# GpSimd normalises the head outputs ahead of k's low parts, q's high part comes two exponentials later, and the maxima's rows are copied from one head's block

## The chip, the cores and the metric

The kernel runs on one core of a Trainium2 chip. The metric is the device time of one execution in microseconds. Before the change it is 1233.8 us (median of three runs, 1231.41 to 1234.8).

## The reference

A transformer block on x (16 sequences of 256 tokens, 512 wide) with cross-attention to ctx, then a feed-forward net with simulated quantisation:

```
q = rope(layernorm(x) @ wq.T); k = rope(ctx @ wk.T); v = ctx @ wv.T     # 16 heads of 32
scores = q_h @ k_h.T * sqrt(32), -inf where |query - key| > 128
x = x + softmax(scores) @ v_h -> (256, 512) @ wo.T + wo_b
h = gelu(quant16(layernorm(x)) @ quant8(W_in) + b_in)                   # 2048 wide, erf gelu
out = x + quant16(h) @ quant8(W_out) + b_out
```

quant16 scales by the largest absolute value of the whole tensor, quant8 by that of each hidden unit in the weights.

## The kernel before, in words

Each engine has its own instruction stream, written out by hand, and semaphores between them. Work on one engine is done strictly in the order written, a wait included.

**Part one, attention**, is 16 steps, one per sequence (`step(b, ...)`, one function per engine). In step b three sequences are in the works: the scores and softmax of b, the projections of b + 1, and the output product and residual of b − 1. Products are done in three terms of high and low parts (`split3`), so each operand has a `_hi` (a rounded copy by ScalarE) and a `_lo` (the rest, by VectorE or GpSimd).

- First half of a step, TensorE: scores of 16 heads two at a time (L604), between them the k, q and v products of b + 1 (L521 to L523) and the transposes of normalised x (`x_transposes`, L533). VectorE takes the row maxima of each head (L1191) and between them the reciprocals of the softmax denominators of b − 1 (`invert`, L1232, out to `neg_max`, whose memory it shares as `den_r`), t_lo for x (L1224), the rotation of k (L1214 to L1217) and the normalisation of oT (`normalise`, L1238).
- The shares: SyncE stores the reciprocals to DRAM (L356), waits for that, and loads them spread over the partitions into `share` (L359), which lies in the first two slots of `probs`. oT times share is the normalised head output. ScalarE rounds it to t_hi (`ot_lead`, L937), GpSimd takes the rest, t_lo (`ot_rest`, L1516), and TensorE multiplies both with wo (`o_products`, L588).
- Middle: VectorE negates the row maxima and splits them (`split_max`, L1196 and L1198), TensorE takes four output products and then transposes the maxima (L616), ScalarE copies them in two pieces to the rows MROW and up of `q_st` for heads 0 to 3 (`max_copy`, L953), and SyncE copies those rows to the other 12 heads (`stack_max`, L350).
- Second half, TensorE: transposed scores (L638, two matmuls per head) with the remaining output products between them, and after heads 7, 11 and 15 and at the end a clump of weighted sums (L652) and denominators (L665) for four heads. ScalarE: 16 exponentials (L960), and among them the high part of q for b + 1 (L906) and of ctx for b + 2 (L911). GpSimd: a band mask on each exponential (`band`, L1528), and among them q's four low parts (L1505) and ctx's four (L1511). VectorE: rotation of q, residual, layer-norm sums, a row block of W_in quantised, layer norm of x for b + 2, the largest value (`largest`, L1162).
- SyncE's queue in step b: load x_res (L325), the shares (L356, L359), x (L319), the maxima's rows, then, once k's low parts and later q's low parts are done, the stacks of k and q for b + 1 (L343; 24 transfers), a block of W_in (L333) and ctx (L315) among them, and the store of x1 (L329). The next step's x_res waits until that store has landed.

GpSimd in the first half: wo_b onto x_res (`bias_x`, L1521), k's low parts (L1505), t_lo.

**Part two** multiplies by W_in and takes the gelu. **Part three** multiplies by W_out: per chunk of 128 hidden units ScalarE scales (L1109) and rounds (L1100), VectorE makes integers (L1459) and the low part g_lo (L1483), TensorE does eight matmuls (L857), and GpSimd adds b_out to four blocks of each tile of x1 (`bias_tile`, L1568).

Of the kernel before, what the change touches and what calls it, by code (L numbers as in the profile page):

```python
# [29 lines left out]
P = 128  # L30
# [55 lines left out]
def build(nc, t):  # L86
# [12 lines left out]
    with ExitStack() as ctx:  # L99
# [212 lines left out]
        def _(sp):  # L312
# [33 lines left out]
            def stack_max(b):  # L346

                sp.wait_ge(mT_done, MAX_COPIES * (b + 1))
                for i in range(1, NC4):
                    sp.dma_start(q_st[MROW:P, KC * i:KC * (i + 1)].bitcast(F32),  # L350
                                 q_st[MROW:P, 0:KC].bitcast(F32)).then_inc(max_stacked[i - 1], 16)

# [164 lines left out]
        def _(pe):  # L517
# [7 lines left out]
            def x_transposes(j, s):  # L525

                if s == 0:
                    pe.wait_ge(ln1_norm, 2 * j + 2)
                    wait(pe, wt_done, j - 1)
                    wait(pe, den_done, j - 1)  # L530
                    wait(pe, rope_step["q"], ROPE_OPS * j)
                for c in range(KC):
                    mm = pe.transpose(q_bank[s][:, c * P:(c + 1) * P], x_ln[:, s, c * P:(c + 1) * P], ident[:])  # L533
                mm.then_inc(xt_mm, 1)
# [365 lines left out]
        def _(act):  # L900
# [95 lines left out]
            def step(b, par, has_c, has_o, has_proj, has_xt):  # L996
# [14 lines left out]
                for n in range(H):  # L1011
                    softmax_exp(b, n)
                    if n == 4 and has_proj:
                        split_hi("q", b + 1)
                    if n == 8 and has_xt:
                        ctx_hi(b + 2)
# [117 lines left out]
        def _(dve):  # L1134
# [59 lines left out]
            def split_max(b):  # L1194
                dve.wait_ge(max_done, 2 * H * (b + 1))
                dve.tensor_scalar(neg_max[:, :, MROW:MROW + H].bitcast(F32R), row_max[:], -1.0, None, ALU.mult).then_inc(msplit, 1)  # L1196
                dve.wait_ge(msplit, 2 * b + 1)
# [32 lines left out]
            def invert(b):  # L1230
                dve.wait_ge(den_mm, NC4 * (b + 1))
                dve.reciprocal(den_r, den_bank[:, 0:S]).then_inc(den_done, 1)  # L1232

            def normalise(b, half):
                dve.wait_ge(oT_out, 2 * b + half + 1)
                dve.wait_ge(share_in, 16 * (b + 1))
                part = oT[:, 2 * half:2 * half + 2].rearrange("p i t -> p (i t)")
                dve.tensor_tensor(part, part, share[:, 2 * half * S:2 * (half + 1) * S], ALU.mult).then_inc(onorm, 1)  # L1238

# [62 lines left out]
            def step(b, par, has_c, has_o, has_proj, has_xt):  # L1302

                between = {p: [] for p in range(H // 2)}
                if has_o:
                    between[0] += [lambda: invert(b - 1)]
                    between[5] += [lambda: normalise(b - 1, 0), lambda: normalise(b - 1, 1)]
                if has_proj:
# [191 lines left out]
        def _(pool):  # L1500
# [12 lines left out]
            def ot_rest(j, s):  # L1513
                pool.wait_ge(ot_hi, 2 * j + s + 1)
                tok = slice(s * P, (s + 1) * P)
                pool.tensor_tensor(t_lo[:, :, tok], oT[:, :, tok], t_hi[:, :, tok].bitcast(F32), ALU.subtract).then_inc(ot_lo, 1)  # L1516

            def bias_x(j):
                pool.wait_ge(xres_in, 16 * (j + 1))
                for s in range(2):  # L1520
                    pool.tensor_tensor(x_res[:, s], x_res[:, s], wo_b[:], ALU.add).then_inc(xres_b, 1)  # L1521
# [14 lines left out]
            def step(b, par, has_c, has_o, has_proj, has_xt):  # L1536
                if has_o:
                    bias_x(b - 1)
                if has_proj:
                    for c in range(KC):  # L1540
# [4 lines left out]
                for n in range(H):  # L1545
                    band(b, n)
                    if 4 <= n < 8 and has_proj:
                        split_lo("q", b + 1, n - 4)
                    if n in (8, 9, 10, 11) and has_xt:
                        ctx_lo(b + 2, n - 8)  # L1550

# [13 lines left out]
            def bias_tile(i, par):  # L1565
                pool.wait_ge(xc_in[par], 8 * i + (16 if par == 0 else 8))
                for u in range(SUB):
                    pool.tensor_tensor(xq[:, par, u], xq[:, par, u], b_out[:], ALU.add).then_inc(xc_b, 1)  # L1568

# [33 lines left out]
```

## Time and profile before

| | us |
|---|---|
| median of three runs | 1233.8 |
| the profiled execution | 1233.87 |
| its span in the trace | 1232.2 |
| TensorE busy | 1148.4 (93%) |
| VectorE busy | 984.4 (80%) |
| ScalarE busy | 640.7 (52%) |
| GpSimd busy | 367.7 (30%) |

The mean granted TensorE clock is 0.985 of full. TensorE's and VectorE's shares are means over three parts. In the 572 us from 128 to 700 of the span, which hold steps of part one alone, TensorE is busy for 537.79 us and VectorE for 507.73, ScalarE for 259.83 and GpSimd for 261.33. In the last 248 us (part three) they are busy for 237.46, 200.91, 177.83 and 48.86. Matmuls are pipelined, so that busy TensorE is not TensorE at its peak. What releases an engine at each step is to be read from the waits and the chain, not from these shares.

### The profile page before, as it was taken

Reading aid. Unit: us, or ns where it says so; the run is one execution under the profiler, and the core shown is the slowest. Engines: PE = TensorE matmul, PEld = TensorE weight load, DVE = VectorE, ACT = ScalarE, POOL = GpSimd, SP = SyncE. Lnnn points to the kernel's source line nnn. Section 1 sums busy time; section 2 is a strip of 40 time slices with the busy share of each in tenths; the row PEclk is TensorE's granted clock in tenths of the full one; section 3 lists DMA queues with packets and bytes.
Section 4 is the critical chain, followed back from the end, with each engine's and each line's share of the span. In section 5 each row is a group of like instructions: output and inputs, shape, how many; then the busy total and the mean of one; then the engine's idle time right before and its main releaser. Section 6 shows DMA issues by size and latency. Waiting matters only on the chain.

```text
span 1232.2 us, 23572 instructions
## 1 busy us (share of the span) xinstructions
PE 1148.4 (93%) x7884; PEld 770.6 (63%) x7928; DVE 984.4 (80%) x2541; ACT 640.7 (52%) x1001; POOL 367.7 (30%) x540
## 2 busy tenths in 40 slices
PE   6989999999999999999999767999999989999998
PEld 6867777876787787687677545444444444444443
DVE  6868889989888988988988746666666688888886
ACT  5254355345335434534533433655556457777775
POOL 1135346345434624634553331000000030121230
PEclk9989999999999999999999969999999999999999
DMA  8463574565466456457545622555554400677762
GB/s 270 124 143 108 162 180 128 143 176 146 126 176 159 121 151 180 131 141 193 132 122 142 180 82 77 175 207 202 203 195 145 150 4 30 186 223 236 239 223 95
DMA packets 95916, 191.12 MB, mean 155 GB/s; under 512 B 13377, under 2 KB 24769, under 8 KB 95809
## 3 DMA queue, kind: packets, MB, share of 16 engines
q1 hardware_dynamic: 95808, 189.75, 52.2%
q8 instruction: 60, 0.98, 0.4%
q14 instruction: 48, 0.39, 0.1%
HBM read 89.16 MB, written 43.91 MB: 108 GB/s over the span
## 4 chain that ended last, share of the span: by engine, by line
DVE 35%; PE 35%; issue 24%; DMA 2%; ACT 1%; SPq 1%; POOL 0%; DVEq 0%; POOLq 0%; ACTq 0%
PE bank L857 17%; DVE bank L1191 7%; PE bank L521 4%; PE bank L522 4%; PE bank L523 4%; DVE bn L1137 3%; DVE roped L1217 2%; DVE rt L1214 2%; PE bank L604 2%; DVE rt L1215 2%; DVE row_max L1191 2%; DVE neg_max L1232 2%; DVE x_res L1184 2%; PE bank L533 1%; DVE nt_t L292 1%
## 5 line engine op out<-in xcount | busy, mean ns | idle before, releaser
L1191 DVE CUSTOM_DVE_ANT_0 bank<-bank,mask 128x256 f32<-128x256 f32 x512 | 201.6, 455 | 52.1 <-PE bank L604 45.3
L857 PE MATMUL bank<-wout_int,g_lo 128*128 128x512 bf16 x512 | 193.5, 379 | 1.1
L857 PE MATMUL bank<-wout_int,g_hi 128*128 128x512 bf16 x491 | 185.7, 379 | 4.3 <-DVE g_lo L1483 4.0
L818 PE MATMUL bank<-qT_lo,win_int 128*128 128x512 bf16 x496 | 188.0, 379 | 1.2
L818 PE MATMUL bank<-qT_hi,win_int 128*128 128x512 bf16 x474 | 179.6, 379 | 0.0
L960 ACT ACTIVATE probs<-bank 128x512 f32<-128x512 f32 x256 | 142.9, 603 | 50.4 <-PE bank L638 46.1
L1528 POOL TENSOR_SCALAR_AFFINE_SELECT probs<-probs 128x256 f32<-128x256 f32 x256 | 109.9, 433 | 82.8 <-ACT probs L960 79.1
L1483 DVE TENSOR_TENSOR g_lo<-h_int,g_hi 128x512 f16<-128x512 f32 x128 | 104.2, 814 | 34.4 <-ACT g_hi L1100 34.0
L604 PE MATMUL bank<-k_st,q_st 96*128 96x256 f32 x512 | 97.7, 303 | 22.6 <-DVE row_max L1191 20.9
L1521 POOL TENSOR_TENSOR x_res<-x_res,wo_b 128x512 f32<-128x512 f32 x32 | 42.0, 1334 | 237.6 <-DMA x_res<-in_x 230.2
L638 PEld LDWEIGHTS bank<-q_st,k_st 128*128 128x128 f32 x512 | 91.2, 194 | 31.0 <-issue 13.6
L1068 ACT ACTIVATE h_ring<-bank,b_in,g_scale 128x512 f32<-128x512 f32 x96 | 73.1, 779 | 71.2 <-PE bank L818 54.1
L1425 DVE TENSOR_REDUCE hmax<-h_ring 128x512 f32 (+1 forms) x96 | 63.4, 683 | 57.3 <-ACT h_ring L1068 55.0
L638 PE MATMUL bank<-q_st,k_st 128*128 128x256 f32 x512 | 104.7, 295 | 2.3 <-ACT probs L960 1.1
L604 PEld LDWEIGHTS bank<-k_st,q_st 96*128 96x128 f32 x512 | 75.8, 193 | 47.4 <-DVE row_max L1191 33.0
L1100 ACT CAST g_hi<-h_int 128x512 f16<-128x512 f32 x128 | 78.9, 617 | 42.6 <-PE bank L857 31.1
L1568 POOL TENSOR_TENSOR xq<-xq,b_out 128x512 f32<-128x512 f32 x32 | 48.5, 1546 | 154.2 <-DMA xq<-x_scratch 147.0
L857 PEld LDWEIGHTS bank<-wout_int,g_hi 128*128 128x128 f16 x512 | 50.0, 98 | 66.3 <-issue 6.4
L857 PEld LDWEIGHTS bank<-wout_int,g_lo 128*128 128x128 f16 x512 | 50.1, 98 | 59.8 <-DVE g_lo L1483 0.2
L652 PE MATMUL bank<-probs,v_sb 128*32 128x256 f32 x1024 | 69.4, 388 | 18.1 <-ACT probs L960 12.0
L818 PEld LDWEIGHTS bank<-qT_lo,win_int 128*128 128x128 bf16 x496 | 48.5, 98 | 57.8
L818 PEld LDWEIGHTS bank<-qT_hi,win_int 128*128 128x128 bf16 x496 | 48.5, 98 | 57.7
(170 smaller groups left out, 2712.9 us busy)
## 6 DMA issues: line engine op xcount, KB each, us to landing
hidden_scratch<-h_ring SPq DMA_DIRECT2D x96, 256.0 KB, 2.0
h_ring<-hidden_scratch SPq DMA_DIRECT2D x96, 256.0 KB, 2.9
k_st<-k_hi SPq DMA_DIRECT2D x128, 128.0 KB, 2.6
q_st<-q_hi SPq DMA_DIRECT2D x128, 128.0 KB, 2.4
xq<-x_scratch SPq DMA_DIRECT2D x16, 1024.0 KB, 6.1
x_ln<-in_x SPq DMA_DIRECT2D x16, 512.0 KB, 4.6
ctx_raw<-in_ctxT SPq DMA_DIRECT2D x16, 512.0 KB, 5.0
k_st<-k_lo SPq DMA_DIRECT2D x64, 128.0 KB, 2.8
```

What stands on the lines that cost most here:

```text
L604: mm = pe.matmul(ring[n % 2][:, qb * S:(qb + 1) * S], q_st[0:MROW, n, qb * P:(qb + 1) * P], k_st[0:MROW, n], start=True, stop=True)
L638: mm = pe.matmul(third[n][:, kb * S:(kb + 1) * S], k_st[:, n, kb * P:(kb + 1) * P], q_st[:, n], start=True, stop=True)
L652: mm = pe.matmul(pv_bank[i // 2][DK * c:DK * (c + 1), (i % 2) * S:(i % 2 + 1) * S], v_sb[:, par, kb, n], probs[:, n % SLOTS, kb], start=kb ...
L818: mm = pe.matmul(bank[f % 4][:], win_int[:, c, f * P:(f + 1) * P], part[:, par, c], start=c == 0 and part is qT_hi, stop=c == KC - 1 and p ...
L857: return pe.matmul(bank[4 * par + u][:], part[:, f % 4, u * P:(u + 1) * P], wout_int[:, f], start=f == 0 and part is g_hi, stop=f == FC - ...
L960: act.activation(probs[:, n % SLOTS].rearrange("p k q -> p (k q)"), third[n][:], ACT.Exp, scale=SCORE_SCALE).then_inc(exp_done, 1)
L1068: act.activation(dst, bank[f % 4][:], ACT.Gelu, bias=b_in[:, f:f + 1], scale=g_scale[:, f:f + 1]).then_inc(gelu_done, 1)
L1100: act.copy(g_hi[:, f % 4], h_int[:, f % 4]).then_inc(ghi_done, 1)
L1191: dve.tensor_tensor_reduce(sc, sc, mask[:, (1 - qb) * P:(1 - qb) * P + S], 1.0, NEG, ALU.add, ALU.max, row_max[:, qb, n:n + 1]).then_inc(m ...
L1425: dve.tensor_reduce(hmax[:, bass.ds(FC * n + f, 1)], src, AX_X, ALU.max, apply_absolute_value=True).then_inc(hmax_done, 1)
L1483: dve.tensor_tensor(g_lo[:, f % 4], h_int[:, f % 4], g_hi[:, f % 4], ALU.subtract).then_inc(glo_done, 1)
L1528: pool.affine_select(out=far, in_=far, compare_op=ALU.is_ge, fill=0.0, base=1 - P, pattern=[[0, 2], [1, P]], channel_multiplier=1).then_in ...
```

## The change

1. The normalisation of oT by the shares goes from VectorE (behind head 11's row maxima) to GpSimd, between `bias_x` and k's low parts. VectorE's `split_max` gets an explicit wait for the store of the reciprocals, as both use `neg_max`.
2. ScalarE makes q's high part behind exponential 6 in place of 4, ctx's behind 9 in place of 8; GpSimd's q low parts go behind bands 6 to 9 (from 4 to 7), ctx's behind 10 to 13 (from 8 to 11).
3. The first half of x's transposes no longer waits for the reciprocal; the second does, whose bank it is.
4. `stack_max` waits only for the first of ScalarE's two copies and reads head 0's rows four times over, in place of reading heads 0 to 3.
5. In part three each of GpSimd's adds of b_out waits for a chunk of its own, 6, 8, 10 or 12 of the tile.

```diff
             def stack_max(b):
-                sp.wait_ge(mT_done, MAX_COPIES * (b + 1))
+                sp.wait_ge(mT_done, MAX_COPIES * b + 1)
                 for i in range(1, NC4):
                     sp.dma_start(q_st[MROW:P, KC * i:KC * (i + 1)].bitcast(F32),
-                                 q_st[MROW:P, 0:KC].bitcast(F32)).then_inc(max_stacked[i - 1], 16)
+                                 q_st[MROW:P, 0:1].bitcast(F32).to_broadcast([P - MROW, KC, S])).then_inc(max_stacked[i - 1], 16)
...
                 if s == 0:
                     pe.wait_ge(ln1_norm, 2 * j + 2)
                     wait(pe, wt_done, j - 1)
+                    wait(pe, rope_step["q"], ROPE_OPS * j)
+                else:
                     wait(pe, den_done, j - 1)
-                    wait(pe, rope_step["q"], ROPE_OPS * j)
...
-                    if n == 4 and has_proj:
+                    if n == 6 and has_proj:
                         split_hi("q", b + 1)
-                    if n == 8 and has_xt:
+                    if n == 9 and has_xt:
                         ctx_hi(b + 2)
...
             def split_max(b):
                 dve.wait_ge(max_done, 2 * H * (b + 1))
+                wait(dve, den_out, 16 * b)
...
-            def normalise(b, half):
-                dve.wait_ge(oT_out, 2 * b + half + 1)
-                dve.wait_ge(share_in, 16 * (b + 1))
-                part = oT[:, 2 * half:2 * half + 2].rearrange("p i t -> p (i t)")
-                dve.tensor_tensor(part, part, share[:, 2 * half * S:2 * (half + 1) * S], ALU.mult).then_inc(onorm, 1)
...
-                    between[5] += [lambda: normalise(b - 1, 0), lambda: normalise(b - 1, 1)]
...
+            def normalise(j, half):
+                pool.wait_ge(oT_out, 2 * j + half + 1)
+                pool.wait_ge(share_in, 16 * (j + 1))
+                part = oT[:, 2 * half:2 * half + 2].rearrange("p i t -> p (i t)")
+                pool.tensor_tensor(part, part, share[:, 2 * half * S:2 * (half + 1) * S], ALU.mult).then_inc(onorm, 1)
...
                 if has_o:
                     bias_x(b - 1)
+                    normalise(b - 1, 0)
+                    normalise(b - 1, 1)
...
-                    if 4 <= n < 8 and has_proj:
-                        split_lo("q", b + 1, n - 4)
-                    if n in (8, 9, 10, 11) and has_xt:
-                        ctx_lo(b + 2, n - 8)
+                    if 6 <= n < 10 and has_proj:
+                        split_lo("q", b + 1, n - 6)
+                    if 10 <= n < 14 and has_xt:
+                        ctx_lo(b + 2, n - 10)
...
                 for u in range(SUB):
+                    pool.wait_ge(hint_done, FC * i + 6 + 2 * u)
                     pool.tensor_tensor(xq[:, par, u], xq[:, par, u], b_out[:], ALU.add).then_inc(xc_b, 1)
```

GpSimd's instructions of one step, from the residual's bias on (x_res; k_lo and q_lo are low parts, t_lo is that of oT, AFFINE_SELECT is the band of one head). Before:

```order
L1521 TENSOR_TENSOR x_res<-x_res,wo_b 128x512 x2
L1505 TENSOR_TENSOR k_lo<-roped,k_hi 128x256 x4
L1516 TENSOR_TENSOR t_lo<-oT,t_hi 128x4x128 x2
L1528 AFFINE_SELECT probs<-probs 128x256 x5
L1505 TENSOR_TENSOR q_lo<-roped,q_hi 128x256
```

And after the change, whose line numbers differ:

```order
L1522 TENSOR_TENSOR x_res<-x_res,wo_b 128x512 x2
L1517 TENSOR_TENSOR oT<-oT,probs 128x512 x2
L1500 TENSOR_TENSOR k_lo<-roped,k_hi 128x256 x4
L1511 TENSOR_TENSOR t_lo<-oT,t_hi 128x4x128 x2
L1529 AFFINE_SELECT probs<-probs 128x256 x7
L1500 TENSOR_TENSOR q_lo<-roped,q_hi 128x256
```

The two multiplications of oT by the shares (in `probs`) now stand ahead of k's low parts, and seven bands instead of five ahead of q's first low part.

ScalarE's instructions in the second half of a step, from the maxima's two copies into q_st. Before:

```order
L953 CAST q_st<-bank 32x512 x2
L960 ACTIVATE probs<-bank 128x512 x5
L906 CAST q_hi<-roped 128x1024
L960 ACTIVATE probs<-bank 128x512 x4
L911 CAST cT_hi<-ctx_raw 128x1024
```

And after:

```order
L954 CAST q_st<-bank 32x512 x2
L961 ACTIVATE probs<-bank 128x512 x7
L907 CAST q_hi<-roped 128x1024
L961 ACTIVATE probs<-bank 128x512 x3
L912 CAST cT_hi<-ctx_raw 128x1024
```

q's rounding moved behind two more exponentials, ctx's behind one more.

## Rows read from the trace of the kernel before

**Rows 1.** The page, chain that ended last, by engine

```profile
DVE 35%; PE 35%; issue 24%; DMA 2%; ACT 1%; SPq 1%; POOL 0%; DVEq 0%; POOLq 0%; ACTq 0%
```

**Rows 2.** Line L1232: duration ns min/median/max, first and last start

```profile
L1232 DVE RECIPROCAL neg_max<-bank x15: 1752/1753/1758, 86.9 to 699.7; 128x256 f32<-128x256 f32 x15
```

**Rows 3.** Chain that ended last, 390 to 440: start us, us, what

```profile
411.06 0.14 DVE oT L1238
...
434.11 0.73 DVE dmax L1162 x2
...
436.93 1.62 DVE neg_max L1232
```

**Rows 4.** TensorE in order of time: start, us, instructions, [idle before, releaser]

```profile
395.18 1.06 PE L533 MATMUL bank<-ident,x_ln 128*128 128x128 f32 x8 [0.47 <-DVE neg_max L1232]
...
414.31 0.47 PE L588 MATMUL bank<-wo_hi,t_hi 128*128 128x512 f32 x1
...
415.87 0.44 PE L616 MATMUL bank<-ident,neg_max 128*128 128x128 f32 x2 [0.39 <-DVE neg_max L1198]
...
422.50 1.07 PE L652 MATMUL bank<-probs,v_sb 128*32 128x256 f32 x16 [0.80 <-ACT probs L960]
...
432.42 1.07 PE L652 MATMUL bank<-probs,v_sb 128*32 128x256 f32 x16 [0.33 <-POOL probs L1528]
```

**Rows 5.** GpSimd in order of time: q's last low part in three steps

```profile
250.28 0.74 POOL L1505 TENSOR_TENSOR q_lo<-roped,q_hi 128x256 fp32r<-128x256 f32 x1
...
425.49 0.74 POOL L1505 TENSOR_TENSOR q_lo<-roped,q_hi 128x256 fp32r<-128x256 f32 x1
...
469.11 0.74 POOL L1505 TENSOR_TENSOR q_lo<-roped,q_hi 128x256 fp32r<-128x256 f32 x1
```

**Rows 6.** SyncE's queue: issue of the shares' load behind each of these

```profile
274.14 0.58 SPq L359 DMA_DIRECT2D probs<-den_scratch  x1
...
447.03 0.58 SPq L359 DMA_DIRECT2D probs<-den_scratch  x1
...
491.87 0.58 SPq L359 DMA_DIRECT2D probs<-den_scratch  x1
```

**Rows 7.** Line L359, the shares' load

```profile
DMA to landing us min/median/max: 3.4/3.8/4.6
```

**Rows 8.** VectorE in order of time, the normalisation

```profile
410.91 1.29 DVE L1238 TENSOR_TENSOR oT<-oT,probs 128x512 f32<-128x512 f32 x2
```

**Rows 9.** GpSimd in order of time, k's low parts and the first t_lo

```profile
408.00 2.83 POOL L1505 TENSOR_TENSOR k_lo<-roped,k_hi 128x256 fp32r<-128x256 f32 x4 [1.71 <-ACT k_hi L906]
412.93 1.27 POOL L1516 TENSOR_TENSOR t_lo<-oT,t_hi 128x512 fp32r<-128x512 f32 x1 [2.11 <-ACT t_hi L937]
```

**Rows 10.** Line L1521: duration ns min/median/max

```profile
L1521 POOL TENSOR_TENSOR x_res<-x_res,wo_b x32: 1262/1292/1760, 95.0 to 750.8; 128x512 f32<-128x512 f32 x32
```

**Rows 11.** Part three: TensorE's waits (page and timeline), VectorE's integers

```profile
L857 PE MATMUL bank<-wout_int,g_hi 128*128 128x512 bf16 x491 | 185.7, 379 | 4.3 <-DVE g_lo L1483 4.0
...
1016.69 0.38 PE L857 MATMUL bank<-wout_int,g_hi 128*128 128x512 bf16 x1 [1.19 <-DVE g_lo L1483]
...
1050.65 0.48 DVE L1459 TENSOR_SCALAR h_int<-h_int,wout_man 128x512 f32<-128x512 f32 x1
...
1054.45 1.49 DVE L1459 TENSOR_SCALAR h_int<-h_int,wout_man 128x512 f32<-128x512 f32 x1
```

**Rows 12.** ScalarE in order of time, exponentials 5 to 7

```profile
421.76 1.57 ACT L960 ACTIVATE probs<-bank 128x512 f32<-128x512 f32 x3
```

**Rows 13.** VectorE in order of time, the last step's normalisation

```profile
718.82 1.29 DVE L1238 TENSOR_TENSOR oT<-oT,probs 128x512 f32<-128x512 f32 x2 [8.38 <-DMA probs<-den_scratch]
```

**Rows 14.** Step 0: TensorE's wait; windows of 5 us, PEclk after POOL's column

```profile
64.72 0.44 PE L616 MATMUL bank<-ident,neg_max 128*128 128x128 f32 x2 [2.08 <-DVE neg_max L1198]
...
65.00:70.00 5.00, 3.90 (x16) 3.21 (x14) 4.76 (x9) 3.77 (x8) 1.91 (x4) 0.52 0.47 105
70.00:75.00 5.00, 4.27 (x35) 2.08 (x34) 4.16 (x11) 2.38 (x4) 4.42 (x8) 0.50 0.60 136
```

## The prediction

> **What bounds the kernel now.** I read the page first. Its chain of what ended last is 35% VectorE and 35% TensorE, with GpSimd at 0% [rows 1]. The kernel has three parts: attention, about 745 us of the span in 16 steps, the first feed-forward product, and the second. The change lies in the attention steps and, by one wait, in the last part. The starts of the 15 reciprocals of the denominators stand 14 steps apart, from 86.9 to 699.7, which gives 43.8 us per step [rows 2]. I take the step around 393 to 437 as the pattern.
>
> Next I read the chain inside that step [rows 3]. It runs through VectorE's tail behind the row maxima (the last work is `largest` at 434.1) to the next reciprocal at 436.9; from a reciprocal it passes to TensorE's transposes of x, which waited for it (395.18) [rows 4], along TensorE, and back into VectorE's row maxima, with the normalisation of oT inside at 411. So VectorE and TensorE hand over to each other. TensorE's own waits in a step are small [rows 4]: 0.47 us for the reciprocal, 0.39 us for the negated maxima ahead of their transposes (they start at 415.87; I call this moment M), 0.80 us for an exponential, 0.33 us for GpSimd's last band.
>
> Last I looked for a loop which isn't on that chain but is almost as long. GpSimd ends q's last low part at 425.49 + 0.74 = 426.2 [rows 5]; then SyncE's queue issues q's stacks, one weight row block, ctx, more stacks, the store of x1, and behind it the load of x_res, the reciprocals' store and, once that has landed, the broadcast load of the shares, at 447.03 [rows 6], which lands in a median 3.8 us [rows 7]. So the shares are in 447.0 + 3.8 − 426.2 = 24.6 us behind q's low parts. In the step after it is 491.87 + 3.8 − 469.85 = 25.8, and in the worst step 274.14 + 3.8 − 251.0 = 26.9 [rows 5, 6]. I take 25.5. Today the normalisation starts at 410.9 [rows 8], and the shares of that step landed before it (the step after: 447.0 + 3.8 = 450.8, against 410.9 + 43.6 = 454.5), so there are 3.7 us of slack, and 3.7 − (26.9 − 24.6) = 1.4 in the worst step. The profile does not show this slack as a wait; the question is whether the change eats it.
>
> **The change part by part.**
>
> *Normalisation to GpSimd.* VectorE loses two instructions, 1.2 us per step [rows 3, 8]. GpSimd gains two 128x512 instructions with two SBUF inputs. The nearest row is its own t_lo, 1.27 us each [rows 9]; its add of x_res and wo_b goes from 1.26 to 1.76 [rows 10]. Bounds 2.5 and 3.5 us for the pair; I take 2.55, since beside it VectorE only runs row maxima. They are put ahead of k's four low parts (2.83 us) on an engine that works in order, and behind these comes t_lo [rows 9]. What follows the landing of the shares was 1.3 (VectorE, both halves) + 0.7 (ScalarE's t_hi, which GpSimd's t_lo waited for) + 1.3 (first t_lo) = 3.4 us with the semaphores. It becomes 2.55 + 2.83 + 1.27 + 0.15 = 6.8 us, because k's low parts can't start before the shares are in. t_hi on ScalarE hides behind k's low parts. TensorE's first output product needs this first t_lo: it starts at 414.31, right at t_lo's end at 414.2 [rows 4, 9].
>
> In a sentence of its own: the Trainium skill (SBUF — State Buffer, "Who interferes with whom") says that a VectorE instruction with at most one SBUF input does not contend with GpSimd, and one with two does. By it the row maxima (one PSUM, one SBUF input) leave the pair at 2.5; if they did contend as in the 1.76 row, it would be 3.5 and the sum 13 us more. Rows bear out the contention at least: with GpSimd's add beside it, VectorE's 0.48 us tensor_scalar took 1.49 [rows 11].
>
> *q's high part behind exponential 6.* It starts 0.98 us later (two exponentials at a pitch of 0.49, three of them in 1.57) [rows 12], and GpSimd's q_lo, and with it SyncE's whole queue, start later too. GpSimd does the bands of 5 and 6 ahead, which it had to do between before, so q's last low part ends about 0.75 us later, 11.1 us behind M instead of 10.36 (426.23 − 415.87). Bounds 0 and 0.98. TensorE's wait of 0.80 for exponential 5 goes, but the last clump then waits for GpSimd's band 15, today's end of 432.4 [rows 4], whose engine has the same work: it ends some 0.15 us earlier, so that is what remains of the 0.80. ctx's later low parts end just as SyncE's queue comes to its load: no charge.
>
> *x transposes.* The first half no longer waits for the reciprocal; by the time of the second it is ready: 0.47 us of TensorE's wait gone.
>
> *Maxima's rows.* The three copies can be issued after ScalarE's first copy, half a microsecond sooner, in 1 KB pieces in place of 4 KB. The nearest broadcast load lands in 3.4 to 4.6 us [rows 7]; scores need it about 3 us after issue, so it costs between 0 and 1 us a step, and I take 0, because it moves a quarter of the bytes of that load. The wait of the negation for den_out is long fulfilled: 0.
>
> *Bias in the last part.* TensorE waits 4.0 us in all for g_lo there, 1.19 us at a time, while GpSimd adds two tiles' bias in a row [rows 11]. Spread over the chunks, these waits go: −4 us (bounds 0 and −4).
>
> **The sum.** Loop one, TensorE and VectorE: 43.8 − 0.47 − 0.15 and about 0.5 of the 1.2 us of normalisation (the rest is lost since TensorE still has v's products there) gives 42.65. Loop two, M to M: 11.1 + 25.5 + 6.8 + 1.05 (four output products ahead of the transposes) = 44.45 us. The second is longer, and longer than today's 43.8, so it sets the step: 0.65 × 13 = +8.5. The first step with a normalisation still gains 1.2. The last step waits 8.38 us for the shares today [rows 13], with nothing to hide in: +0.75 for q and +1.3 for the slower engine, +2. The last part −4. Together +5.3: this is the profiled execution's 1233.9 (its span is 1232.2) to 1239, and that execution stands within 0.1 us of the median 1233.8.
>
> But in this loop TensorE stands idle in front of the output products: today it is through its scores 414.31 − 372.25 = 42.1 us behind the last M (43.62 us before this one), then 42.1 − 0.47 − 0.15 − 0.7 = 40.7 (0.7 for its own waits on the row maxima behind the normalisation), and t_lo comes at 11.1 + 25.5 + 6.8 = 43.4: 2.7 us, 1.8 to 4.1 by the step. In step 0 it waited 2.08 us at this same place, and the granted clock was at half (0.52 and 0.50, 1.2 of 2.4 GHz) for the next 10 us [rows 14]. A fall would hit the output products and the transposed scores, some 7 us of TensorE work that is then on the loop. Bounds per fall 0 and 7; I take 3, as TensorE has no gaps there and the clock came back under work in rows 14. I expect four falls in 13 steps, where the idle time is above average: +12. Forecast 1251.
>
> A sentence apart: the Trainium skill (TensorE: Matmul & The Clock Gate, "Part 1: The HAM clock gate") calls the half rate the default that activity lifts; what rows 14 show agrees.
>
> **The rivals.**
> 1. *Faster.* The queue loop is shorter than I make it, by 1.5 us or more (transfers land sooner when they fall in quieter stretches, or q's low parts end no later), so the first loop sets the step: 42.65, −1.1 × 14 = −15, and −4: 1215. For it: of today's slack of 1.4 to 3.7 us most steps have 2.5 or more. Against it: 0.75 + 3.4 us are added. If the loop is only 0.7 shorter, it is 1228.
> 2. *The loop, but no fall of the clock*: 1239. For it: TensorE's waits of 0.3 to 0.8 us in each step do not move the clock, and it is not shown where between these and 2.08 it falls. Against it: step 0.
> 3. *The clock falls in nearly every step*: 1239 + 13 × 3 = 1278. For it: each step has the same idle place. Against it: half of them are shorter than step 0's.
> 4. *No change that counts*: the added 0.65 per step is 0, and the gains of the last part meet the last step's loss, 1232.
>
> **How the numbers follow.** Forecast 1251 with 0.42, rival 1 0.20, rival 2 0.20, rival 3 0.10, rival 4 0.08. The range is 1224 to 1275: it takes in rival 2 and 4 and the near half of rival 1, and stops short of 3; the likeliest case's own range is 1242 to 1264. Within 0.3% (3.7 us, about what a measurement of this kernel can tell from no change) is rival 4 and a little of the others: 0.10; faster 0.20, slower 0.70.
>
> **What would show it.** Right: steps of 44.4 us or more; GpSimd waits for the shares, TensorE's idle time ahead of L588 is named and ends with GpSimd's t_lo, VectorE has idle time in its row maxima, and the granted clock dips in some steps. Also no wait over 1 us for g_lo in the last part. Wrong: steps of 42.7 us, with the chain still through VectorE's tail, or a share that lands before 24 us. If q's last low part ends at M + 10.4, that step was wrong alone.

## The result, and the profile after

| | before | after |
|---|---|---|
| median | 1233.55 us (1231.41 to 1234.8, 4 runs) | 1251.11 us (1246.93 to 1256.15, 4 runs) |
| ratio after / before | | 1.0142, 95% interval 1.0117 to 1.0168 |
| profiled execution, its span | 1233.9, 1232.2 | 1256.15, 1254.3 |
| reciprocal to reciprocal, mean of 14 steps | 43.77 | 45.46 |
| mean granted clock, 128 to 680 | 1.00 | 0.98 |

The change makes the kernel 17.6 us slower; 1251 was forecast. The profiled execution of after is the longest of its four, 5 us above the median. It also has the lowest mean granted clock over its whole span, 0.971; the other three have 0.974, 0.974 and 0.977. So its steps show more of the loss than the median has.

The page's chain of what ended last, by engine; beside [rows 1], VectorE has fallen from 35% to 28%, and DMA and SyncE's queue have grown from 2% and 1%:

```profile
PE 38%; DVE 28%; issue 24%; DMA 4%; SPq 3%; POOL 1%; ACT 1%; DVEq 0%; POOLq 0%
```

The line of the reciprocals, which answers to [rows 2]. (722.8 − 86.4) / 14 gives 45.46 us per step:

```profile
L1234 DVE RECIPROCAL neg_max<-bank x15: 1750/1752/1756, 86.4 to 722.8; 128x256 f32<-128x256 f32 x15
```

The chain inside a step, where before it was VectorE's tail [rows 3]. It now runs through the queue's transfers and GpSimd's normalisation to TensorE's output products (start us, us, what):

```profile
315.39 4.56 DMA x_scratch<-x_res
...
320.45 3.87 DMA den_scratch<-neg_max
...
324.34 3.53 DMA probs<-den_scratch
...
328.01 2.54 POOL oT L1517 x2
...
331.73 2.88 issue
334.60 2.05 PE bank L589 x4
```

The 2.88 us of "issue" are TensorE's wait, in which GpSimd does k's low parts and the first t_lo.

GpSimd in order of time, from the end of one step into the next: q's last low part, then the work behind the shares. The columns are those of [rows 4]:

```profile
438.93 0.73 POOL L1500 TENSOR_TENSOR q_lo<-roped,q_hi 128x256 fp32r<-128x256 f32 x1
...
464.53 2.52 POOL L1517 TENSOR_TENSOR oT<-oT,probs 128x512 f32<-128x512 f32 x2 [1.64 <-DMA probs<-den_scratch]
467.01 2.81 POOL L1500 TENSOR_TENSOR k_lo<-roped,k_hi 128x256 fp32r<-128x256 f32 x4
469.78 2.51 POOL L1511 TENSOR_TENSOR t_lo<-oT,t_hi 128x512 fp32r<-128x512 f32 x2
```

TensorE at the output products and the transposes of the negated maxima (M), in that step and in the one before it:

```profile
427.08 0.47 PE L589 MATMUL bank<-wo_hi,t_hi 128*128 128x512 f32 x1 [2.37 <-issue]
...
428.33 0.44 PE L617 MATMUL bank<-ident,neg_max 128*128 128x128 f32 x2
...
471.15 0.47 PE L589 MATMUL bank<-wo_hi,t_hi 128*128 128x512 f32 x1 [1.25 <-issue]
472.62 0.44 PE L617 MATMUL bank<-ident,neg_max 128*128 128x128 f32 x2 [0.30 <-DVE neg_max L1200]
```

M to M is 472.62 − 428.33 = 44.3 us, and its pieces can be read off: 439.66 − 428.33 = 11.3 from M to the end of q's last low part; 464.53 − 439.66 = 24.9 to the start of the normalisation, 0.14 us behind the landing of the shares; 471.15 − 464.53 = 6.6 to the first output product; 1.47 to the next M. GpSimd stood idle 1.64 us for the shares, TensorE 1.25 to 2.37 us for GpSimd. In before no engine waited for the shares but in the last step. The shares' load itself lands as before (us, min/median/max), beside [rows 7]:

```profile
DMA to landing us min/median/max: 3.4/3.8/5.1
```

The same waits added up over the whole program (us, times, longest):

```profile
PE bank L589 <- issue: 31.6, 14, 3.9
POOL oT L1517 <- DMA probs<-den_scratch: 23.9, 15, 3.0
```

So TensorE stands 31.6 / 14 = 2.26 us per step in front of the output products. "issue" names no releaser, but each of these waits ends as the first t_lo ends.

The granted clock, in windows of 5 us (columns as in [rows 14]) around the longest of these waits, 3.9 us, and in the step after it:

```profile
285.00:290.00 5.00, 2.07 (x8) 1.78 (x9) 4.80 (x10) 0.96 (x3) 4.07 (x5) 0.90 0.00 0
290.00:295.00 5.00, 5.00 (x23) 4.25 (x23) 3.03 (x5) 3.13 (x7) 1.51 (x4) 0.76 0.35 82
330.00:335.00 5.00, 1.36 (x7) 1.10 (x7) 4.45 (x14) 1.62 (x3) 5.00 (x7) 0.83 0.00 0
335.00:340.00 5.00, 5.00 (x16) 4.02 (x16) 3.42 (x6) 1.66 (x3) 0.74 (x1) 0.50 0.16 39
```

TensorE works 2.07 and 1.36 of 5 us, and the clock then goes to half (1.2 of 2.4 GHz). There are eight such falls between step 0 and the last, each in or behind one of the waits, of 2.08 to 3.94 us. Two waits of 2.28 and 2.37 us have none behind them, nor have the waits of 1.92 us and less.

The last step, GpSimd and TensorE, beside [rows 13]. The wait for the shares is 1.60 us now, but the first output product comes 25.49 us behind the reciprocal, where it came 22.64 behind before:

```profile
743.74 2.48 POOL L1517 TENSOR_TENSOR oT<-oT,probs 128x512 f32<-128x512 f32 x2 [1.60 <-DMA probs<-den_scratch]
...
748.31 0.77 PE L589 MATMUL bank<-wo_hi,t_hi 128*128 128x512 f32 x1 [11.80 <-ACT t_hi L938]
```

The last part is better, as meant. In place of the 4.3 us of [rows 11] TensorE waits 0.4 us:

```profile
L858 PE MATMUL bank<-wout_int,g_hi 128*128 128x512 bf16 x491 | 185.8, 379 | 0.4 <-issue 0.2
```

### The profile page after: what moved, and what is told of

It is laid out like the page before. It is cut to its first block, busy times and chain, and to the rows that moved or that the text cites. A ratio compares the mean times of both kernels' runs of the same rounds, so it can differ in the third digit from the quotient of the medians.

```text
span 1254.3 us, 23605 instructions
## 1 busy us (share of the span) xinstructions
PE 1154.3 (92%) x7884; PEld 779.9 (62%) x7928; DVE 985.3 (79%) x2511; ACT 641.3 (51%) x1001; POOL 395.6 (32%) x570
## 4 chain that ended last, share of the span: by engine, by line
PE 38%; DVE 28%; issue 24%; DMA 4%; SPq 3%; POOL 1%; ACT 1%; DVEq 0%; POOLq 0%
PE bank L858 17%; DVE bank L1192 4%; PE bank L589 4%; PE bank L521 3%; PE bank L522 3%; PE bank L523 3%; DVE bn L1138 3%; SPq L343 2%; DVE roped L1219 2%; PE bank L605 2%; PE bank L639 2%; DVE rt L1217 2%; DVE rt L1216 2%; DVE nt_t L292 1%; DVE neg_max L1234 1%
## 5 line engine op out<-in xcount | busy, mean ns | idle before, releaser
L1529 POOL TENSOR_SCALAR_AFFINE_SELECT probs<-probs 128x256 f32<-128x256 f32 x256 | 106.8, 421 | 89.5 <-ACT probs L961 85.1
L1522 POOL TENSOR_TENSOR x_res<-x_res,wo_b 128x512 f32<-128x512 f32 x32 | 43.8, 1390 | 254.8 <-DMA x_res<-in_x 247.4
L1478 DVE TENSOR_TENSOR g_lo<-h_int,g_hi 128x512 f16<-128x512 f32 x128 | 89.1, 696 | 41.4 <-ACT g_hi L1101 37.8
L639 PEld LDWEIGHTS bank<-q_st,k_st 128*128 128x128 f32 x512 | 94.1, 197 | 31.3 <-issue 13.6
L1101 ACT CAST g_hi<-h_int 128x512 f16<-128x512 f32 x128 | 78.9, 617 | 47.2 <-PE bank L858 43.1
L1572 POOL TENSOR_TENSOR xq<-xq,b_out 128x512 f32<-128x512 f32 x32 | 41.5, 1296 | 166.5 <-ACT h_int L1110 166.5
L589 PE MATMUL bank<-wo_hi,t_hi 128*128 128x512 f32 x120 | 53.7, 447 | 43.4 <-issue 31.6
```

The lines of the kernel that those rows point to most:

```text
L589: mm = pe.matmul(kv_bank[s][:], part[:, c, tok], (w_hi if w == "hi" else w_lo)["wo"][:, c], start=c == 0 and m == 0, stop=c == KC - 1 and ...
L639: mm = pe.matmul(third[n][:, kb * S:(kb + 1) * S], k_st[:, n, kb * P:(kb + 1) * P], q_st[:, n], start=True, stop=True)
L1101: act.copy(g_hi[:, f % 4], h_int[:, f % 4]).then_inc(ghi_done, 1)
L1478: dve.tensor_tensor(g_lo[:, f % 4], h_int[:, f % 4], g_hi[:, f % 4], ALU.subtract).then_inc(glo_done, 1)
L1529: pool.affine_select(out=far, in_=far, compare_op=ALU.is_ge, fill=0.0, base=1 - P, pattern=[[0, 2], [1, P]], channel_multiplier=1).then_in ...
```

## The experiments

Ratios are to the kernel before, measured beside each on the same chip. The first experiment below and the third to fifth stand beside 1232.3 us, on one chip; the others beside 1233.1 or 1233.3 us, on another. A difference between two experiments from different chips carries that 1 us as well. Theory A is the prediction's: q's low parts, SyncE's queue, the shares' bounce and GpSimd's work behind it form a loop longer than the step, and the clock falls in TensorE's waits on it.

**The change with the normalisation back on VectorE.**

```diff
+                    between[5] += [lambda: normalise(b - 1, 0), lambda: normalise(b - 1, 1)]
...
                 if has_o:
                     bias_x(b - 1)
-                    normalise(b - 1, 0)
-                    normalise(b - 1, 1)
```

> The changed kernel with the normalisation back on VectorE, behind head 11's row maxima; all else of the change stays. Theory A (the loop through SyncE's queue, the shares and GpSimd sets the step because the normalisation and k's low parts follow the shares on GpSimd): share landed to first output product goes from 6.8 back to 3.4 us, the loop is 11.3 + 25.5 + 3.4 + 1.05 = 41.3 us and no longer binds; the step is that of before less 0.47 and 0.15, about 43.1, no fall of the clock from the steps before the last, part three keeps its 4 us: 1222 us (1218 to 1228). Theory B (q's later high part and the copies in 1 KB pieces are what costs): stays at 1245 or more. Theory C (gain of VectorE's relief is real and only the clock costs): VectorE is 1.2 us longer per step, about 1235.

Measured: 1229.59 us (1227.62 to 1231.69, 10 runs), ratio 0.9969 [0.9956, 0.9982]. All of the loss goes, and with it every fall of the clock between step 0 and the last. So the normalisation's place is a necessary part of the loss. But 1222 (1218 to 1228) was expected, and the step is (698.8 − 85.5) / 14 = 43.80, no shorter than before. VectorE in order of time shows a part of the reason, in the layer norm ahead of the reciprocal:

```profile
475.31 0.66 DVE L293 SCALAR_TENSOR_TENSOR rstd<-nt_t,rstd 128x2 f32<-128x2 f32 x1
476.00 0.32 DVE L291 TENSOR_TENSOR nt_t<-rstd 128x2 f32<-128x2 f32 x1
476.36 0.33 DVE L292 SCALAR_TENSOR_TENSOR nt_t<-nt_t,veps 128x2 f32<-128x2 f32 x1
476.72 0.16 DVE L293 SCALAR_TENSOR_TENSOR rstd<-nt_t,rstd 128x2 f32<-128x2 f32 x1
```

and beside it GpSimd:

```profile
474.16 0.73 POOL L1513 TENSOR_TENSOR cT_lo<-ctx_raw,cT_hi 128x256 fp32r<-128x256 f32 x1
...
475.23 0.72 POOL L1513 TENSOR_TENSOR cT_lo<-ctx_raw,cT_hi 128x256 fp32r<-128x256 f32 x1
475.90 0.77 POOL L1530 TENSOR_SCALAR_AFFINE_SELECT probs<-probs 128x256 f32<-128x256 f32 x2
```

These instructions work on two elements per partition. One takes 0.66 us beside a low part and ends with it (475.31 + 0.66 = 475.97; the low part, 475.23 + 0.72 = 475.95). The two beside the two bands take 0.32 and 0.33, and the one behind them 0.16. GpSimd's low parts now end later, so more of the iteration lies beside them. Its 11 small instructions (L285 to L293) take 5.12 us from the first to the last in 13 steps; in the kernel before it is 4.54 (5.11 in one step). In the last step, where GpSimd stands idle beside them, the same 11 on 128x4 elements take 2.14. From the negated maxima to the next reciprocal is 21.66 us here.

**That kernel with q's and ctx's parts in their old places too** (before, then, with the early transposes of x, the small copies of the maxima, and the spread bias). Further edit:

```diff
-                    if n == 6 and has_proj:
+                    if n == 4 and has_proj:
                         split_hi("q", b + 1)
-                    if n == 9 and has_xt:
+                    if n == 8 and has_xt:
                         ctx_hi(b + 2)
...
-                    if 6 <= n < 10 and has_proj:
-                        split_lo("q", b + 1, n - 6)
-                    if 10 <= n < 14 and has_xt:
-                        ctx_lo(b + 2, n - 10)
+                    if 4 <= n < 8 and has_proj:
+                        split_lo("q", b + 1, n - 4)
+                    if n in (8, 9, 10, 11) and has_xt:
+                        ctx_lo(b + 2, n - 8)
```

> The changed kernel with two parts undone: the normalisation on VectorE and q's and ctx's parts at their places of before (so before plus x's transposes without the reciprocal, the earlier 1 KB copies and the spread bias). In the trace of the run with the normalisation alone undone, VectorE's tail, from the negated maxima to the next reciprocal, is 21.66 us in place of 21.17, though it has the same instructions. Theory D: that is GpSimd's later low parts, which lie beside VectorE's small instructions of the layer norm; with them early the tail is 21.2 again and the step 21.85 + 21.2 = 43.05 us: 14 x 0.7 = 10 and 4 of part three less than before: 1219 us (1215 to 1223). Rival: the tail is longer for another reason (x's transposes, copies): stays at 1229.

Measured: 1221.38 us (1220.11 to 1223.1, 4 runs), ratio 0.9910 [0.9887, 0.9932]: better than both kernels. The step is (690.6 − 86.1) / 14 = 43.18, the way from the negated maxima to the reciprocal 21.15, and of the same iteration the last instructions are short again (the 11 together 4.53 us):

```profile
469.56 0.33 DVE L293 SCALAR_TENSOR_TENSOR rstd<-nt_t,rstd 128x2 f32<-128x2 f32 x1
469.92 0.16 DVE L291 TENSOR_TENSOR nt_t<-rstd 128x2 f32<-128x2 f32 x1
470.12 0.16 DVE L292 SCALAR_TENSOR_TENSOR nt_t<-nt_t,veps 128x2 f32<-128x2 f32 x1
```

So the later places of q's and ctx's parts cost 1229.6 − 1221.4 = 8.2 us even where the normalisation is on VectorE (7.3 by the ratios, as the two ran on different chips). The iteration's share of it is (5.12 − 4.53) × 13 = 7.7 us; that GpSimd's instructions are what lengthens it is read from where they end, not tried by itself.

**Before with the normalisation on GpSimd, nothing else** (but the wait that `split_max` then needs).

```diff
                 dve.wait_ge(max_done, 2 * H * (b + 1))
+                wait(dve, den_out, 16 * b)
...
-                    between[5] += [lambda: normalise(b - 1, 0), lambda: normalise(b - 1, 1)]
...
                 if has_o:
                     bias_x(b - 1)
+                    normalise(b - 1, 0)
+                    normalise(b - 1, 1)
```

> The kernel before with only the normalisation moved to GpSimd ahead of k's low parts. Theory A: loop of 10.36 + 25.5 + 6.8 + 1.05 = 43.7 us on average beside about 43.3 for the TensorE and VectorE loop; steps with late shares wait up to 1.5 us more, TensorE idles 1 to 2 us ahead of the output products, few falls of the clock; last step +1.3: 1236 us (1231 to 1243). Theory B: faster than before, about 1227.

Measured: 1238.51 us (1236.77 to 1240.03, 7 runs), ratio 1.0041 [1.0027, 1.0056]. As A said: the slack of 1.4 to 3.7 us is used up. Reciprocals from 85.1 to 703.4 make the step 44.16, TensorE now waits ahead of its output products, and the clock falls twice:

```profile
PE bank L588 <- issue: 13.9, 12, 2.6
```

**The change with q's and ctx's parts in their old places.** The edit is that of the second experiment, on after.

> The changed kernel with q's high part back behind exponential 4, ctx's behind 8 and GpSimd's low parts back at their bands. Theory A: SyncE's queue starts about 0.96 us earlier (M + 10.36 in place of M + 11.3), 13 times: loop 43.7, fewer falls of the clock; 1251 - 12 - some 5 for falls = 1234 us (1228 to 1240). Theory B' (the late q parts do not matter for the loop): 1250, and TensorE's wait of 0.8 us for an exponential is back.

Measured: 1237.83 us (1231.22 to 1242.49, 10 runs), ratio 1.0041 [1.0018, 1.0064]. The step is 44.12 and the wait ahead of the products 20.4 us; four falls. With the normalisation on GpSimd, then, q's earlier parts shorten the step from 45.46 to 44.12. Counted from the fastest kernel (the second experiment), the normalisation on GpSimd costs 1237.8 − 1221.4 = 16.4, q's and ctx's later parts 8.2, both 1251.1 − 1221.4 = 29.7. The same move made in the kernel before, the third experiment, costs only 1238.5 − 1232.3 = 6.2: that kernel's step is longer to begin with (43.77 for 43.18), so the same loop lies less far above it. And though this kernel has the early transposes and the spread bias, which are gains elsewhere, it is no faster than that one: TensorE arrives earlier and waits longer (20.4 for 13.9 us), with four falls for two.

**Idle matmuls in TensorE's wait, against the falls.** The change with 16 matmuls of 256 columns on idle data ahead of the output products, in 13 steps.

```diff
+                    if s == 0 and has_proj and j < NB - 3:
+                        pe.wait_ge(rope_step["k"], ROPE_OPS * (j + 3))
+                        for _ in range(16):
+                            pe.matmul(kv_bank[0][:, 0:S], idle_b[:, 0:P], idle_b, start=True, stop=True)
```

> The changed kernel with 16 extra bf16 matmuls of 256 columns (about 1.8 us, results never read) on TensorE into the bank of the output products, where it idles ahead of them, in 12 of the 14 steps. If the falls of the granted clock cost what is over the loop's 44.45 us: clock at 1.00 over these steps, each step 44.2 to 45 without the outliers of 46 and 47.7; 1241 us (1237 to 1245). If the falls cost nothing (the loop hides them): unchanged at 1251, with the clock at 1.00. If the fillers themselves get in the way: above 1255.

Measured: 1244.76 us (1240.71 to 1247.68, 4 runs), ratio 1.0085 [1.0053, 1.0118]. The windows' line of the steps, here and for after, shows the clock back at 1.00 from 0.98:

```profile
128.00:680.00 552.00, 523.88 (x4508) 429.84 (x4507) 492.24 (x1423) 245.94 (x416) 274.87 (x410) 1.00 0.55 149
```

```profile
128.00:680.00 552.00, 504.24 (x4244) 411.14 (x4243) 488.34 (x1400) 245.04 (x415) 272.22 (x408) 0.98 0.54 145
```

Between the medians the falls cost 1251.1 − 1244.8 = 6.4 us; the intervals of the two ratios, some 3 and 4 us to each side, touch, so that is 6 with an error of about 5. The two profiled executions differ by 1256.15 − 1244.57 = 11.6. Only in that one of after are the falls counted: eight, and here one is left, at 689 us, in a step without idle matmuls. The loop without falls holds the step at (711.2 − 86.6) / 14 = 44.62:

```profile
L1238 DVE RECIPROCAL neg_max<-bank x15: 1748/1750/1755, 86.6 to 711.2; 128x256 f32<-128x256 f32 x15
```

What one fall costs can be read inside after: M to M is 44.91 us on average in the six steps that have no fall around their first M, and 46.15 in the seven that have one, though the way from q's low parts to the shares is 25.5 in both. So a fall costs about 1.2 us of the step behind it.

The idle matmuls cost a little themselves. In six of their steps they are still running when the first t_lo ends, and the first output product comes 0.2 to 0.7 us behind it in place of 0.1, 2 us in all. So the falls cost a little more than the difference, and the loop alone is a little shorter than 44.62.

**k's low parts ahead of the normalisation.** If the loop is that long because k's 2.8 us stand behind the shares, they can go in front.

```diff
                 if has_o:
                     bias_x(b - 1)
-                    normalise(b - 1, 0)
-                    normalise(b - 1, 1)
                 if has_proj:
                     for c in range(KC):
                         split_lo("k", b + 1, c)
                 if has_o:
+                    normalise(b - 1, 0)
+                    normalise(b - 1, 1)
                     ot_rest(b - 1, 0)
                     ot_rest(b - 1, 1)
```

> The changed kernel with k's low parts ahead of the normalisation on GpSimd. Share landed to first output product then has 2.55 + 0.7 + 1.27 + 0.15 = 4.7 us, but the normalisation can't start before k's low parts end, 17.2 us behind the reciprocal, so the first output product comes at 17.2 + 2.55 + 0.7 + 1.27 + 0.15 = 21.9 us and the step is about 44.2 us whenever the shares are in by 17.2, which they are. TensorE idles about 1.3 us ahead of the products, so few or no falls of the clock. Theory A (it is the order behind the shares): 1238 us (1234 to 1243), no step over 45. Rival (GpSimd's added 2.5 us costs wherever they stand): 1248 or more.

Measured: 1251.93 us (1251.27 to 1256.04, 4 runs), ratio 1.0168 [1.014, 1.0196]. I had 1238; the rival held. GpSimd in order of time shows the normalisation no longer waits for the shares, but for k's low parts ahead of it, and these for ScalarE's k_hi:

```profile
462.34 2.82 POOL L1500 TENSOR_TENSOR k_lo<-roped,k_hi 128x256 fp32r<-128x256 f32 x4 [1.71 <-ACT k_hi L907]
465.12 2.53 POOL L1517 TENSOR_TENSOR oT<-oT,probs 128x512 f32<-128x512 f32 x2
468.38 2.51 POOL L1511 TENSOR_TENSOR t_lo<-oT,t_hi 128x512 fp32r<-128x512 f32 x2 [0.73 <-ACT t_hi L938]
```

and t_hi, hidden behind k's low parts in after, now adds its 0.73. TensorE's wait is still there, under another name (11.6 us of it in the last step, so 2.2 in each other):

```profile
PE bank L589 <- ACT t_hi L938: 42.6, 15, 11.6
```

**The same with the idle matmuls**, to tell the order from the clock: the edits of the last two together.

> The kernel with k's low parts ahead of the normalisation on GpSimd (1251.9 us, six falls of the clock in the steps), with the 16 idle matmuls of 256 columns ahead of the output products. If falls of the clock are what brought that kernel above its expected 1238: no falls, 1241 us (1238 to 1246). If it is the loop itself (reciprocal, GpSimd's bias, k's low parts, normalisation, t_lo) at 45 us a step: 1248 or more with the clock at 1.00.

Measured: 1247.53 us (1246.08 to 1248.56, 4 runs), ratio 1.0115 [1.0084, 1.0146], a step of 44.81, and one fall between step 0 and the last, again where no idle matmuls stand. So with this order too it is mainly the work in a row, not the clock, that makes the step: k_hi, four k_lo, the pair, t_hi and t_lo.

**The bias of the last part spread, nothing else** (before with one added wait on GpSimd).

```diff
+                    pool.wait_ge(hint_done, FC * i + 6 + 2 * u)
```

> The kernel before with only the spread bias of part three. The four waits of TensorE for g_lo (0.39 and three of 1.19 us) go: 4 us less than before, 1228.3 us. Rival: VectorE is held up elsewhere in the tile instead, beside its results, and the waits come back: no change.

Measured: 1228.32 us (1225.76 to 1231.7, 10 runs), ratio 0.9965 [0.9949, 0.9982]: −4.8 us against 1233.1. The prediction's four waits go; 4.8 is a little over its bound of 4.

**The change with the old copies of the maxima's rows.**

```diff
-                sp.wait_ge(mT_done, MAX_COPIES * b + 1)
+                sp.wait_ge(mT_done, MAX_COPIES * (b + 1))
...
-                                 q_st[MROW:P, 0:1].bitcast(F32).to_broadcast([P - MROW, KC, S])).then_inc(max_stacked[i - 1], 16)
+                                 q_st[MROW:P, 0:KC].bitcast(F32)).then_inc(max_stacked[i - 1], 16)
```

> The changed kernel with the copies of the maxima's rows as before (4 KB pieces, behind both of ScalarE's copies). Theory A: no part of the loop: 1251 us within the scatter of its runs (1246 to 1256). Theory B (1 KB pieces slow the queue): 3 us or more faster. Rival B' (the earlier issue is worth something): 3 us or more slower.

Measured: 1255.01 us (1253.52 to 1258.89, 4 runs), ratio 1.0195 [1.0169, 1.0221]. Its range overlaps that of after, 1246.9 to 1256.2, so the 4 us between the medians are not shown to be the copies'. The same edit on the fastest kernel:

> The fastest so far (1221.4 us: the changed kernel with the normalisation on VectorE and q's and ctx's parts at their old places) with the copies of the maxima's rows as before the change. If the copies, issued 0.55 us later and in 4 KB pieces, are hidden behind the scores of heads 0 to 3: 1221 us (1219 to 1224). If heads 4 and on wait for them: 0.3 to 0.5 us in 14 steps, 1226 to 1229.

Measured: 1223.41 us (1220.86 to 1225.2, 4 runs), ratio 0.9911 [0.9877, 0.9945], where the new copies gave 1221.38. The ranges overlap, so four runs show no difference; that the new copies gain up to 2 us there isn't ruled out.

## Why the prediction was right, point by point

**The slack used up: right.** The main step of the prediction was that a loop behind q's low parts, which no wait shows in before, decides once the change has lengthened it. The third and fourth experiments show it. M to M was put at 44.45: with the falls kept away the step measures 44.62, and in after M to M is 44.25 to 45.89, mean 44.91, in the six steps that have no fall around their first M. With the normalisation on VectorE the loop doesn't decide, late parts or not: in the first experiment no engine waits for the shares before the last step, and they land 0.4 to 3.3 us before they are used. There q's later parts cost by another way, told below.

**The terms of the loop.** Predicted, and measured in after:

| piece | predicted | measured |
|---|---|---|
| M to the end of q's last low part | 11.1 | 11.3 without a fall, 11.5 to 12.8 with one |
| to the landed shares | 25.5 | 24.7 to 26.8, mean 25.5 over 13 steps |
| to the first output product | 6.8 | 6.8 |
| product to M | 1.05 | 1.00 to 1.85, mean 1.46 |
| TensorE's wait per step | 2.7 (1.8 to 4.1) | mean 2.26 (0.97 to 3.94) |

The product to M was put 0.4 us too small on average. I had taken the negated maxima as ready. Their two instructions on VectorE now run beside GpSimd's t_lo. The lines of both in after (ns, min/median/max), and in one step:

```profile
L1198 DVE TENSOR_SCALAR neg_max<-row_max x16: 182/854/1206, 64.0 to 740.0; 128x32 fp32r<-128x32 f32 x16
L1200 DVE SCALAR_TENSOR_TENSOR neg_max<-row_max,neg_max x16: 192/1210/1222, 64.2 to 741.0; 128x32 fp32r<-128x32 f32 x16
```

```profile
425.72 2.50 POOL L1511 TENSOR_TENSOR t_lo<-oT,t_hi 128x512 fp32r<-128x512 f32 x2
...
426.33 0.69 DVE L1198 TENSOR_SCALAR neg_max<-row_max 128x32 fp32r<-128x32 f32 x1
427.05 1.22 DVE L1200 SCALAR_TENSOR_TENSOR neg_max<-row_max,neg_max 128x32 fp32r<-128x32 f32 x1
```

and with the normalisation on VectorE (the first experiment), where the second t_lo ends as they start:

```profile
L1198 DVE TENSOR_SCALAR neg_max<-row_max x16: 180/181/182, 63.3 to 723.4; 128x32 fp32r<-128x32 f32 x16
L1200 DVE SCALAR_TENSOR_TENSOR neg_max<-row_max,neg_max x16: 191/193/194, 63.5 to 723.6; 128x32 fp32r<-128x32 f32 x16
```

0.37 us become 1.9 us here, and the second of the two ends with the second t_lo (427.05 + 1.22 = 428.27; 425.72 + 2.50 = 428.22). TensorE's transposes start right behind it, at 428.33, after four products, which at a pitch of some 0.25 would have let them start about 0.2 earlier. This is read from the traces; no run took it away alone. The row maxima of the same stretch keep their 0.38 us apart, so the pair, GpSimd's two multiplications, cost 2.52 us as I had it, not 3.5. The Trainium skill (SBUF — State Buffer, "Who interferes with whom") has both: a VectorE instruction with one SBUF input stays clear of GpSimd, while tensor_scalar in a two-port mode and an instruction with two SBUF inputs don't, and the port that they share is an exclusive lock. I had weighed that rule for the row maxima and not for the two instructions behind them; a duration of 1.22 us, about one t_lo of 1.25, and an end together with it agree with such a lock.

**The clock: right in kind, wrong in number and size.** I expected four falls of 3 us, 12 us in all. The profiled execution has eight, and one costs about 1.2 us of its step (46.15 − 44.91); between the medians all of them cost 6.4 us. The term that was mis-sized is the charge per fall. I had put the slower output products and scores wholly on the loop, but the falls lengthen the way from M to the end of q's last low part by only 0.2 to 1.4 us and that from the first product to M by 0.3 on average. That TensorE has room in the rest of the slow stretch is how I read it; no run tried it. The Trainium skill (TensorE: Matmul & The Clock Gate, "Part 1: The HAM clock gate") says that activity lifts the throttle; the matmuls on idle data, which brought 0.98 to 1.00, agree.

**What made up for it.** Without the falls I had 1239 and the run gives 1244.8. It comes from the loop (14 × (44.62 − 43.77) = 11.9, where I had 0.65 × 13 − 1.2 = 7.3) and the last step (+2.85 for +2), against the last part (−4.8 for −4): 11.9 + 2.85 − 4.8 = 10.0 of the 10.7 between the profiled executions, 1233.87 and 1244.57. So by the medians the total of 1251 is nearer than its parts, and that is luck: 5.8 too little without the falls, 5.6 too much in the clock. In the profiled execution of after the clock's 12 is about met, 11.6, by twice the falls at less than half the price, and the total is 5 too little.

**The first loop: wrong.** I had 42.65 us for it with VectorE relieved, hence 1215 for rival 1; with the normalisation left on VectorE it was 43.1, hence 1222 for the first experiment. It measured 43.80 there, with q later, and 43.18 without. Missing was what GpSimd's later low parts do to VectorE's small instructions: q's part was costed at 0.75 us of the second loop and at a gain of 0.15 for the first. The early transposes and the small copies together bring 1228.3 − 1221.4 = 6.9, near the 0.47 × 14 = 6.6 of the transposes' wait; with the old copies it is 1228.3 − 1223.4 = 4.9, and the two aren't told apart better than that.

**The order on GpSimd: not the cause it looked like.** The 6.8 us behind the shares contain k's 2.83, and it seemed that moving them would give most of it back. It gave nothing, since then the same engine's work in a row, from k_hi on, becomes the chain. The 2.5 us of the pair cost in both places that were tried on this engine.

Rivals 1 (1215), 2 (1239) and 4 (1232) are out by the interval; rival 3, falls in nearly all steps, had the place right, but it is eight steps, at less than half its price. Two sums of the rivals leave out terms of the forecast's own: with the 1.2 of the first step rival 4 is 1231, and a loop that is 0.7 shorter gives 1230, not 1228. Neither bears on the forecast.

## What to carry to other kernels

Before work is moved from a busy engine to an idle one, add up every loop through the idle one, with queue issues and transfers, over one full step: here such a loop of some 40 us had 1.4 to 3.7 us to spare in a step of 43.8, and no wait showed it. Moving 1.3 us of work onto an engine that is busy for 30% of the span, and nothing else, made the kernel 0.4% slower; with q's parts later as well it was 1.4%. Then test each part of a change alone: three parts were worth 12 us together, and the other two, the normalisation's engine and q's and ctx's places, cost 30. Where a total comes out right, look at the parts: by the medians two errors of almost 6 us had cancelled here.

## What the runs showed of the hardware

- Beside GpSimd's instructions VectorE's small ones grow by far more than their size and end together with the GpSimd instruction beside them: a 128x32 tensor_scalar from 0.18 to as much as 1.21 us, the 128x32 two-input one behind it from 0.19 to 1.22, 128x2 ones from 0.16 to 0.66 beside a low part and to 0.32 beside a band (the 11 of the layer norm's iteration to as much as 5.6). The row maxima with one PSUM input did not change.
- GpSimd's 128x512 multiply of two SBUF inputs takes 1.26 us (the pair 2.52) beside VectorE's row maxima; VectorE's own took 1.29 for the pair.
- TensorE's granted clock fell to half (1.2 of 2.4 GHz) eight times behind waits of 2.08 to 3.94 us within steps that were otherwise full of work, but not behind two of 2.28 and 2.37; 16 matmuls of 256 columns on idle data in each wait kept it at 1.00. A fall cost its step only about 1.2 us.
- In the last part, adding the bias at a steadier pace shortened VectorE's g_lo from a mean of 814 to 696 ns and GpSimd's own additions from 1546 to 1296 ns, and gave 4.8 us.
